# Scan and routed attention of a hybrid block: mixing sums added from PSUM, step sizes begun per silu, three norms on ScalarE, keys projected once, output projections in two banks

## The reference, cut to what matters

```
# M: state-space block on 256 inner channels, state size 64
xc, z = split(x @ w_in);  xc = silu(conv4(xc))
Bt, Ct = split(xc @ w_bc);  dt = softplus(xc * w_dt + dt_bias)
h_t = exp(dt_t * A) * h_(t-1) + (dt_t * xc_t) * B_t ;  y_t = h_t . C_t
out = (y + d_skip * xc) * silu(z) @ w_out
# E, E2: routed attention, 16 heads of 64, 4 chosen for each sequence
idx = top4(softmax(mean(x @ Wr + br)))
Q, K, V = (x @ W + b)[heads idx];  O = softmax(Q K^T / 8) V ;  out = O @ Wo + bo
```

## Time and profile before

| | us |
|---|---|
| median of 3 runs (lowest, highest) | 4931.47 (4931.03, 4934.67) |
| profiled execution, its own time | 4937.51 |
| its span | 4936.2 |

### The profile page before, as it was taken

How to read it: one execution, slowest core, us unless ns; L and a number is a source line. 1 busy time by engine, 2 the same in 40 slices (tenths; PEclk the granted TensorE clock), 3 DMA queues, 4 the chain that set the end, 5 groups by cost and what they waited for, 6 DMA issues and landing times.

```text
span 4936.2 us, 79012 instructions
## 1 busy us (share of the span) xinstructions
PE 3892.6 (79%) x31446; PEld 2136.4 (43%) x31446; DVE 3482.2 (71%) x5239; ACT 2994.0 (61%) x4977; POOL 838.2 (17%) x1094
## 2 busy tenths in 40 slices
PE   6888558768789996899998566666666656899998
PEld 4666323222244443667677211111111113667677
DVE  6888566476440005777787899999999995777787
ACT  3444126536533333555565799999999994555565
POOL 2444110000047770000000111111111110000000
PEclk8999659969889998999999555555555558999999
DMA  1000000000032210000000000000000000000000
GB/s 41 1 1 1 1 3 1 1 1 1 19 69 35 34 17 9 2 8 2 2 2 6 1 1 1 1 1 1 1 1 1 1 0 9 2 8 2 2 2 19
DMA packets 50140, 37.86 MB, mean 8 GB/s; under 512 B 25555, under 2 KB 39262, under 8 KB 49758
## 3 DMA queue, kind: packets, MB, share of 16 engines
q1 hardware_dynamic: 49774, 32.82, 3.3%
HBM read 30.58 MB, written 2.23 MB: 7 GB/s over the span
## 4 chain that ended last, share of the span: by engine, by line
PE 54%; DVE 24%; ACT 10%; issue 9%; POOL 1%; SPq 1%; DMA 1%; DVEq 0%; ACTq 0%; POOLq 0%
DVE d_negmax L2332 11%; PE psum L1837 9%; PE psum L1866 9%; PE psum L1852 6%; ACT d_junk L2394 5%; PE psum L1507 5%; PE psum L1530 4%; PE psum L1816 3%; PE psum L1124 2%; PE psum L1113 2%; PE psum L1879 2%; ACT wl_p L1345 2%; PE psum L1098 2%; DVE wl_negmax L1250 1%; PE psum L498 1%
## 5 line engine op out<-in xcount | busy, mean ns | idle before, releaser
L2332 DVE TENSOR_REDUCE d_negmax<-psum 128x1 f32<-128x1024 f32 x1024 | 1183.8, 1213 | 100.2 <-PE psum L2264 100.2
L2394 ACT ACTIVATE d_junk<-psum,d_negmax 128x1024 bf16<-128x1024 f32 x1024 | 1137.8, 1128 | 74.7 <-DVE d_negmax L2332 67.1
L2264 PE MATMUL psum<-d_qT,d_kT 64*128 64x512 bf16 x2048 | 604.3, 599 | 441.3 <-ACT d_junk L2394 424.1
L1981 DVE TENSOR_REDUCE f_m_E<-psum 128x1 f32<-128x1024 f32 x512 | 603.3, 1220 | 59.2 <-PE psum L1837 44.6
L2083 ACT ACTIVATE hidden<-psum,f_nm_E 128x1024 f32<-128x1024 f32 x512 | 566.8, 1115 | 107.5 <-DVE f_nm_E L1984 107.4
L1837 PE MATMUL psum<-f_qk_E 64*128 64x512 f32 x2048 | 555.6, 621 | 8.9 <-ACT hidden L2083 6.9
L1866 PE MATMUL psum<-f_pT_E,f_v_E 128*64 128x128 f32 x8192 | 504.4, 276 | 1.7 <-ACT f_pT_E L2090 1.7
L2000 DVE COPY f_pT_E<-psum 128x512 f32<-128x512 f32 x512 | 352.4, 688 | 193.7 <-PE psum L1852 188.2
L2090 ACT COPY f_pT_E<-psum 128x512 f32<-128x512 f32 x512 | 300.4, 587 | 297.4 <-PE psum L1852 297.4
L2264 PEld LDWEIGHTS psum<-d_qT,d_kT 64*128 64x128 bf16 x2048 | 105.4, 101 | 857.3 <-ACT d_junk L2394 805.6
L1866 PEld LDWEIGHTS psum<-f_pT_E,f_v_E 128*64 128x64 f32 x8192 | 442.7, 137 | 19.3 <-ACT f_pT_E L2090 1.9
(11 more groups left out here) (308 smaller groups left out, 5273.8 us busy)
## 6 DMA issues: line engine op xcount, KB each, us to landing
moe_gates_on_all<-moe_gate_spill SPq DMA_DIRECT2D x8, 2048.0 KB, 15.5
moe_w<-in_moe_w SPq DMA_DIRECT2D x8, 256.0 KB, 4.5
out<-residual SPq DMA_DIRECT2D x1, 2048.0 KB, 8.7
residual<-in_hidden_states SPq DMA_DIRECT2D x2, 768.0 KB, 8.0
f_wqk_E<-in_Wq SPq DMA_DIRECT2D x16, 64.0 KB, 2.2
f_wqk_E<-in_Wk SPq DMA_DIRECT2D x16, 64.0 KB, 2.1
residual<-in_hidden_states SPq DMA_DIRECT2D x2, 256.0 KB, 3.4
m_taps<-in_m_conv SPq DMA_DIRECT2D x4, 128.0 KB
```

The source lines that it names most:

```text
L1981: last = V.tensor_reduce(m2[:, u % 4, f:f + 1], two(2 * f), X, ALU.max)
L2264: last = T.matmul(bank(2 + 2 * (at % 3) + jj), kT[half, s, jb * P:(jb + 1) * P], qT[half, s, c * BANK:(c + 1) * BANK], start=True, stop=True)
L2332: V.tensor_reduce(mh[:, t % 2, n // 2, n % 2:n % 2 + 1], two(2 + 2 * (at % 3)), X, ALU.max, negate=True).then_inc(*maxed.up(at))
L2394: A.activation(junk[:, at % 3, :], two(2 + 2 * (at % 3)), ACT.Exp, bias=mh[:, t % 2, n // 2, n % 2:n % 2 + 1], accum_out=sh[:, t % 2, n // ...
```

## The change

**Scan.** `dve_mix` multiplies slots 0 to 3 into `m_z` and slots 4 to 6 in place in PSUM. The additions are now four: three slots of PSUM plus three of `m_z`, back into PSUM; two slots plus two into a new tile `m_z_sums`; and these one by one onto PSUM's slot 6, from which the gate reads. The diagonal term (`dve_skip`) stands ahead of the wait for `pe_mix`. As the banks are in use until the gate has read them, `pe_mix(i)` waits for `y_done(i - 1)` in place of `state_done(i - 1)`. `dve_raw` does each of a group's four steps behind its own silu, and stands ahead of `dve_out`. The norms of channel banks 1 to 3 are eight ACT instructions (Identity with scale and a shift that DVE makes once); the first stays on DVE.

**Routed attention.** Keys are projected once: the two halves of a key bank hold different positions, made by two matmuls of 64 columns of weights, side by side in PE's columns. So a duo has 8 pieces for queries, 4 for keys, 4 for values: 16. The keys' weights are loaded once. The two halves of an output projection go to banks 7 and 6, with no wait between them, one unit earlier (odd units), and the loop is one unit shorter. The value product's first half waits until the residual has taken the projection before it (`summed(t - 1, 1)`), since both use bank 6.

```diff
@@ scan, pe_mix
-                    T.wait_ge(*state_done(i - 1))
+                    T.wait_ge(*state_done(-1))
+                    if i:
+                        T.wait_ge(*y_done(i - 1))
@@ scan, dve_raw
                 def dve_raw(q):
-                    V.wait_ge(*silued(Q4 * q + Q4 - 1))
-                    vstep(V.tensor_tensor(quad(dtx, q), quad(xz, q)[:, :, 0:DI], row(wdt), ALU.mult))
-                    V.tensor_tensor(quad(dtx, q), quad(dtx, q), row(dtb), ALU.add).then_inc(*pre.up(q))
+                    for k in range(Q4 * q, Q4 * q + Q4):
+                        V.wait_ge(*silued(k))
+                        vstep(V.tensor_tensor(dtx[:, k % SLOTS, :], xz[:, k % SLOTS, 0:DI], wdt[:, :], ALU.mult))
+                        last = V.tensor_tensor(dtx[:, k % SLOTS, :], dtx[:, k % SLOTS, :], dtb[:, :], ALU.add)
+                    last.then_inc(*pre.up(q))
@@ scan, dve_mix
-                    V.tensor_tensor(zz[:, s, 0:LV + 1, :], psum[:, 4:8, :].rearrange("p b (l n) -> p (b l) n", l=2)[:, 0:LV + 1, :],
-                                    dec[:, s, 0:LV + 1, :], ALU.mult)
+                    V.tensor_tensor(zz[:, s, 0:4, :], mix[:, 0:4, :], dec[:, s, 0:4, :], ALU.mult)
+                    V.tensor_tensor(mix[:, 4:7, :], mix[:, 4:7, :], dec[:, s, 4:7, :], ALU.mult)
                     vstep(V.tensor_tensor(state[:, :], state[:, :], dec[:, s, 8, :], ALU.mult))
-                    V.tensor_tensor(state[:, :], state[:, :], bank(7)[:, DI:2 * DI], ALU.add).then_inc(*state_done.up(i))
-                    V.wait_ge(*skip_done(i))
-                    V.wait_ge(*gd_done(i))
-                    vstep(V.scalar_tensor_tensor(zz[:, s, 7, :], dtx[:, at, :], gtt[:, r, :], zz[:, s, 7, :], ALU.mult, ALU.add))
-                    for n in (4, 2, 1):
-                        vstep(V.tensor_tensor(zz[:, s, 0:n, :], zz[:, s, 0:n, :], zz[:, s, n:2 * n, :], ALU.add))
+                    V.tensor_tensor(state[:, :], state[:, :], mix[:, 7, :], ALU.add).then_inc(*state_done.up(i))
+                    vstep(V.tensor_tensor(mix[:, 4:7, :], mix[:, 4:7, :], zz[:, s, 0:3, :], ALU.add))
+                    vstep(V.tensor_tensor(zsum[:, :, :], mix[:, 4:6, :], zz[:, s, 3:5, :], ALU.add))
+                    for n in range(2):
+                        vstep(V.tensor_tensor(mix[:, 6, :], mix[:, 6, :], zsum[:, n, :], ALU.add))
@@ scan, act_normed, called at step 2 of a group behind act_y
+                    for n in range(8 * g, 8 * g + 8):
+                        last = A.activation(norm[:, n % 16, :], hid[:, token(n), :], ACT.Identity, bias=shift[:, n:n + 1], scale=n_rs[:, n:n + 1])
@@ routed attention
-            NPIECE, NQK = 20, 16
+            NPIECE, NQK = 16, 12
@@ pe_piece
-                        T.matmul(bank(bk), ws[:, b, kq, 2 * jp + h, :, :], chans[:, b, PAD + g * BANK:PAD + (g + 1) * BANK],
-                                 start=True, stop=True).then_inc(*piece.up(n, m))
+                            for jj in range(2):
+                                last = T.matmul(bank(bk)[64 * jj:64 * jj + 64, :], wk[:, b, 2 * jp + h, :],
+                                                chans[:, b, PAD + (2 * g + jj) * BANK:PAD + (2 * g + jj + 1) * BANK],
+                                                start=True, stop=True, skip_group_check=True, tile_position=(0, 64 * jj))
@@ pe_av, first half
-                            T.wait_ge(*oT_done(t - 1))
+                            T.wait_ge(*summed(t - 1, 1))
@@ pe_project
+                out_at = lambda h: bank(7 - h)[:, h * D:(h + 1) * D]
-                        if h:
-                            T.wait_ge(*proj(t, 0))
-                        T.matmul(bank(bk)[:, h * D:(h + 1) * D], oT[64 * h:64 * h + 64, t % 2, :], wo[64 * h:64 * h + 64, jp, :],
+                        T.matmul(out_at(h), oT[64 * h:64 * h + 64, t % 2, :], wo[64 * h:64 * h + 64, jp, :],
@@ the loops of pe and dve
-                        if u >= 4 and u % 2 == 0:
-                            pe_project((u - 4) // 2)
+                        if u >= 3 and u % 2:
+                            pe_project((u - 3) // 2)
```

More of the change, by code:

```diff
@@ L696, in dve @@
                         q, at = i // Q4 + 1, i % Q4
+                        dve_skip(i)
                         dve_mix(i)
@@ L820, in act @@
                             act_router()
+                        if at == 2 and q % 2 and q // 2 + 1 < NG:
+                            act_normed(q // 2 + 1)
                         if at == 1 and q < NQ:
@@ L1747, in phase_E @@
                 last_bank = []
-                for u in range(NU + 3):
+                for u in range(NU + 2):
                     n = units[min(u, NU - 1)][0]
@@ L2037, in dve @@
                             dve_land(u, 1)
-                        if u >= 4 and u % 2 == 0:
-                            dve_project((u - 4) // 2)
+                        if u >= 3 and u % 2:
+                            dve_project((u - 3) // 2)
                         if u < NU and n == 0 and m > NPIECE:
@@ L2068, in act_piece @@
                     b, jp = duos[n]
-                    g, h, kq = m // 4, m // 2 % 2, m % 2
+                    kind, g, h = qk_piece(m)
+                    kq = int(kind == "k")
                     A.wait_ge(*piece(n, m))
```

80 lines of the change are left out of this document (51 added, 29 removed).

## The result

The changed kernel takes 4852.2 us (median of 4 runs, 4849.0 to 4854.2) against 4933.1 for the kernel before (4 runs): a ratio of 0.9835, 95% interval 0.9818 to 0.9852, 81 us less. The forecast was 4844 us, 88 us less than before. The total is close; its two parts are not. The forecast had 23 us from the scan and 65 from the routed attention. Split by stage, the two traces give 9 and about 80; run one without the other, the parts give 0 and 81.

What follows compares the result with a forecast made beforehand. No one engine bounds the scan; PE bounds attention units with pieces, the scores-maxima-exponentials chain those without. Scan 23 plus attention 65 is 88 us off 4931.5: 4844 us, own range 4828 to 4860.

Steps and rivals of the forecast that it cites:

- (a): Scan, DVE's new mixing: nine instructions take 5.9 us against 9.42; the diagonal term, 0.5, counts only where DVE is late.
- (b): Scan, PE's mixing waiting for the last step's gate: covered except at step 2, where step 2 to 3 takes 11.0 us.
- (c): Scan, norms moved to ACT: 5.9 us leave DVE in three groups and cost nothing on ACT; uncovered, 2.4 us a group.
- (d): Scan, raw step size some 2.5 us earlier: counted only at the start, 1.6 us.
- Rival 1: Scan gives nothing, the new wait and lower clock eating what the port gives back: 4867 us; chance 0.2.
- (e): Routed attention, projection's two passes side by side: saves 0.45 us in each tile with pieces, 22 us.
- (f): Routed attention without pieces, additions moved to the tile-closing unit: a pair lasts 10.7 us against 10.88, 12 us in all.
- (g): Routed attention, four pieces fewer: two tiles in each of three duos go from 12.79 to 10.7 us, 25 us.
- (h): Ahead of the routed attention's loop, four pieces fewer: 8 us.
- (i): Routed attention, odd units with value pieces: DVE's work reaches 6.7 us against PE's 6.3, a loss of 2 us.
- Rival 2: Routed attention, column halves don't run side by side in key pieces, costing 31 us: 4875 us; chance 0.06.
- rival 4: Scan's port holds all vanish, PE keeps its clock, and (f) comes at its better end: 4819 us; chance 0.1.

Runs made afterwards that it cites:

- the run of the scan alone: Scan of the changed kernel with the routed attention of the kernel before: 4937.3 us, ratio 1.0000 to the kernel before.
- the split wait: Changed kernel, with PE's mixing waiting for the last step's state, and for its gate only ahead of level 4: 4821.5 us, ratio 0.9762.

## Why the prediction was right, and where it was not

The total was right to 8 us. It was right because two errors of opposite sign, 14 us in the scan by its trace (23 by the run of the scan alone) and 15 in the attention, nearly cancel. That is luck: neither part was right to 8 us, and nothing in the sum ties the one error to the other.

**Scan, (a) the mixing.** The price of its instructions was right to 2% (5.8 against 5.9 us, and writing PSUM costs what reading it costs). Step 1 to 2 was wrong: 15.6 us, forecast 13.7. The step that failed is "plus 0.5" for the diagonal term, and the step size taken over unchanged. With DVE faster, what is behind it comes earlier, POOL's products too; they now meet L649, which takes 1.5 more, and the step size 0.5. Seven groups, 13 us. The forecast counted the ports' holds as gone where operands went to PSUM. They were not gone; they moved to the next instruction with both operands in SBUF.

**(b) the new wait.** The term was 11.0 for step 2 to 3, and 8 us for the clock. The mechanism was named rightly; the size was not. The sum priced a hold of 1.3 that was 0.2, and the lower clock in four groups of eight; the trace has it in six of them (step 2 to 3 lasts 12.4 to 12.9 us in four, 11.3 and 11.9 in two). The 11.0, with the 8 us for the clock spread over eight groups 12.0, came out as 12.4 in most groups. Over the whole scan the two faults cancel: these steps stand 1 us under the forecast. By the Trainium skill (TensorE: Matmul & The Clock Gate, HAM oscillation) gaps in PE's work bring the clock down; the trace agrees with the 4.30 idle and the 5.28 us behind it, and with the split wait, where both are gone. The larger fault is in what was asked. I asked whether the wait is covered, and compared the result with the time before; I didn't ask what step 2 to 3 would be without it. The answer is 8.2, and 24 us of the scan.

**(c) the norms.** The 5.9 us that leave DVE are what they took in each of three groups (5.96). "They cost nothing" held (ACT's 3.2 us a group lie beside other work; the forecast had 2.4). But 17.1 less 11.0 in step 2 to 3 had their gain in it together with that of the additions, and the additions, with their wait, leave nothing to the norms: DVE has 4.9 us to spare there. Alone it was worth 22.9 us. PE's idle of 5.06 in the earlier trace rows, from which the forecast took the loss by the clock, stands behind the norms too: the kernel before has it in the three groups with norms, ahead of the next group's first mixing, and with the norms alone moved no idle ahead of a mixing is over 2.3 us. **(d)** failed in its place: 1.6 us were forecast at the start and nothing behind it. The start can't be read: the first mixing begins at 66.0 to 68.4 us in seven traces with the new raw step size, and at 66.5 to 68.9 in seven with that of before. The run shows 0.9 a group in step 1 to 2, 5.7 in the scan, and nothing in the whole that is outside the intervals.

Added up over steps: 12.7 us in 1 to 2 (7 x 1.9, less for the first), 3 in 0 to 1, 0.8 in 3 to 0, less 3 in the last steps and 1 in 2 to 3. That is, but for rounding, the 12.6 by which 449.1 stands over the forecast's 436.5; another us is the start (0.5 for the forecast 1.6). Rival 1 (the scan gives nothing) named both causes, the hold in what has two operands left (1.5 us a group; it was 2) and the clock in all groups (it was six of eight), and by the run of the scan alone it was the right case for this stage.

**Routed attention.** (e) Side by side was worth 0.55, not 0.45; a tile with pieces falls by 0.54, 48 tiles 26 us, forecast 22. (f) was the mis-sized one: 0.44 a pair without pieces and not 0.18. 68 tiles make 30 us, not 12. The step that failed is "so they start 0.5 later": from the additions' start to the next maximum it is 0.65 (2591.50 to 2592.15), less the 0.28 of idle 0.37, and the trace has 0.32 (5.38 for the odd unit against 5.06). On a gain of 0.2 such a rounding is all. (g) 12 x 2.3 = 28, forecast 25; the keys alone brought 23 in all with (h). (h) 6, forecast 8; a key piece takes 0.97 (1.94 for two), as forecast. (i) No loss shows; the value products waited 2.5 us for the residual in all. The first and the last duos gave less than the middle ones (6.4 and 5.8 against 11.8 us in the first stage), which the forecast had not told apart; that takes 10 off the sum of these terms. Rival 2 (no halves side by side) fell with the 0.97, rival 3 (costly PSUM writes) with the 0.956, rival 4 with the holds that moved.

## What to carry to other kernels

A wait put later to free a buffer must be compared with the version that waits for each part of it, not only with the time before: here a wait for the state ahead of the first four levels, and for the gate only ahead of the last two, was worth 24 us of the scan, and the gain of the norms hid that the new mixing cost more than it gave. Of two edits that relieve the same engine at the same step, price the second with the first done, and by what it takes there: the same eight norms took 5.96 us beside POOL and 2.13 without it. An operand moved out of SBUF did not take the port's hold away here; it passed to the next instruction with two SBUF operands.

## What the runs showed of the hardware

- DVE writing PSUM costs no more than reading it: 768 columns with output and one input in PSUM 956 ns, the same rate (1.04 ns a column and 0.155 us) as 256 or 1792 columns read from it.
- An idle of 3.1 us ahead of the same 8 score products left them at 2.23 us in one kernel and at 3.49 in another; in the scan an idle of 4.30 was followed by the lower level in six groups. In the kernel before an idle of 1.54 us ahead of the mixing's 24 products left them at 2.81 us at one place (169.26) and at 4.49 at another (224.44). So idle can be followed by a slow stretch, and need not be.
- Two 128-column products into two banks, from different halves of the array, let the next products start after 0.27 us; in one bank, one after the other, after 0.82.
- A DVE instruction with one SBUF input and its output in SBUF is held beside POOL too: three norms of 128x128 took 4.25 us beside POOL's products (4.27 us) in the kernel before, and eight took 2.13 us with the norms on DVE in the changed kernel, where POOL stood idle.
